# Normalising behind the statistics on ScalarE alone, with logarithm and exponential from one table set

## The chip, the cores and the metric

One core of a Trainium2 chip. The metric is the device time of one execution in microseconds (us); smaller is better. Engines are named as in the profile: PE is TensorE, PEld its weight loads, DVE VectorE, ACT ScalarE, POOL GpSimd, SP SyncE. Each engine works through its own instruction queue strictly in order; a wait at the head of a queue holds everything behind it.

## The reference, cut to what matters

A graph network of four layers over 6250 nodes with 64 features and 206250 edges (sorted by destination). Per layer, with `msg` an edge's message:

```
msg  = relu(h[src] + edge_attr) + 1e-7
ex   = exp(msg*t - segment_max(msg*t)[dst])
agg  = segment_sum(msg * ex / segment_sum(ex)[dst])
z    = relu(layernorm((h + agg) @ w1 + b1))        # 128 wide: norm 1
h    = h + z @ w2 + b2
next = relu(layernorm(h))                          # 64 wide: norm 2
layernorm(x) = (x - mean) * rsqrt(var + 1e-5) * g + b
```

## The kernel before, in words

`prepare` and the stages after it encode the edges and lay them out (up to 1750 us of the trace). Then `layer` runs three times in a loop (tag `mid`) and once more (tag `last`).

A layer walks over 49 blocks `d` of 128 nodes. The edges of a block lie in slots, one edge of each of the 128 nodes per slot: 32 slots whose source rows come by matmuls with one-hot matrices (`passes`, L1273), and `S.V[d]` more (6 to 39) whose rows POOL gathers from `ztab` with one indirect DMA per slot (`gathers`, L1258). For each block DVE adds both to the encoded edges (`add` L1290, four times; `over` L1302, which waits for the gathers), takes the maximum over slots (`most`, L1309, L1313), subtracts it (`sub`, L1332, two or three slices), ACT takes the exponential (L1338), DVE multiplies (`mul`, L1346), PE sums both over the slots (L1356), and DVE folds the four partial sums (`fold`, L1366).

Odd blocks have many gathered slots, even ones few. Blocks are finished in pairs, (1,2), (3,4) and so on, called units: `node_unit(u)` is a Python generator that issues agg, two matmuls and both norms, cut into steps by `yield`. The order on each queue is set at build time: `steps(n, last)` takes up to `n` steps of the unit between the pieces of the block loop. A `yield "gap"` ends the current call of `steps` early (unless n is 99), so that other work is issued in between. Of one unit, norm 1 is issued from the end of block d (odd) to the adds of d+1, and norm 2 from the first `mul` of block d+1 to the adds and the `over` of d+2.

`norm` (L232 to L265) works on two nodes of a partition at once (columns c = 0, 1): DVE takes statistics (L235, L239) and half the variance (L243), ACT takes `Ln` and `Exp` of [128, 2] for a first root (L246, L248, each with a table load before it), three gaps follow, DVE corrects the root by one Newton step (L253 twice, L257) and forms the shift (L260), and ACT applies both (L263, twice). After norm 2 DVE multiplies and adds the gains (L1439, L1444), then comes L1464 and a chain of ACT casts and DVE subtractions that splits the row in three bf16 parts (L1475, L1479), before POOL writes the row to `ztab` (L1488). In the last layer L1455 and a POOL scatter to the output (L1460) stand in their place, issued within the unit's own step; `fetch_out` (L1525) loads what is added there.

POOL's queue in a layer: at the top of iteration d `gathers(d+1)` (which waits for `over(d-1)`), in the last layer with even d `fetch_out`, then the row writes of finished units.

Of the kernel before, what the change touches and what calls it, by code (L numbers as in the profile page):

```python
# [12 lines left out]
ACT = mybir.ActivationFunctionType  # L13
# [3 lines left out]
LN_EPS = 1e-05  # L17
# [125 lines left out]
def build(nc, S, T):  # L143
    PE, VE, AE, GP, SP = nc.tensor, nc.vector, nc.scalar, nc.gpsimd, nc.sync
# [3 lines left out]
    def sb(name, shape, dt=FP32, ctx=None):  # L148
        return (ctx or top).enter_context(nc.sbuf_tensor(name, shape, dt))

    with top:
# [3 lines left out]
        pe_s, ve_s, ae_s = (next(names) for _ in range(3))  # L155
# [5 lines left out]
        def fresh():  # L161

            return Count(pe_s), Count(ve_s), Count(ae_s)
# [7 lines left out]
        def vwait(value):  # L171
            VE.wait_ge(ve_s, value)
# [22 lines left out]
        mv = sb("mv", [128, 2, 2])  # L195
        nwf = sb("nwf", [128, 8, 2])
        nwi = sb("nwi", [128, 4, 2], I32)

        def rsqrt_steps(V, v, y, f, g, i, w):

            vwait(w)
            k = V(VE.tensor_scalar(i, v.bitcast(I32), 1, None, ALU.logical_shift_right))
            V(VE.tensor_scalar(f, v, -0.5, None, ALU.mult))
            yield
            vwait(k)
            k = V(VE.tensor_scalar(y.bitcast(I32), i, -1, RSQRT_SEED, ALU.mult, ALU.add))
            yield
            for _ in range(3):
                vwait(k)
                if v.shape[-1] == 2:  # L210
                    for c in (0, 1):
                        k = V(VE.scalar_tensor_tensor(g[:, c:c + 1], y[:, c:c + 1],
                                                      f[:, c:c + 1], y[:, c:c + 1],
                                                      ALU.mult, ALU.mult))
                else:
                    k = V(VE.tensor_tensor(g, y, y, ALU.mult))
                    vwait(k)
                    k = V(VE.tensor_tensor(g, g, f, ALU.mult))
                yield
                vwait(k)  # L220
                k = V(VE.scalar_tensor_tensor(y, g, 1.5, y, ALU.add, ALU.mult))
                yield
            return k
# [8 lines left out]
        def norm(V, A, src, width, out):  # L232

            for s in (0, 1):
                q = V(VE.bn_stats(st[:, s, :], src[:, s, 0:width]))  # L235
            yield
            vwait(q)
            for s in (0, 1):
                q = V(VE.bn_aggr(mv[:, s, :], st[:, s, :]))  # L239
            yield  # L240
            vwait(q)
            root, half, by, shift = (nwf[:, i, :] for i in range(4))
            q = V(VE.tensor_scalar(half, mv[:, :, 1], LN_EPS, -0.5, ALU.add, ALU.mult))  # L243

            AE.wait_ge(ve_s, q)
            q = A(AE.activation(by, half, ACT.Ln, scale=-2.0))  # L246
            AE.wait_ge(ae_s, q)
            q = A(AE.activation(root, by, ACT.Exp, scale=-0.5))  # L248
            for _ in range(3):
                yield "gap"  # L250
            VE.wait_ge(ae_s, q)
            for c in (0, 1):
                q = V(VE.scalar_tensor_tensor(by[:, c:c + 1], root[:, c:c + 1], half[:, c:c + 1],  # L253
                                              root[:, c:c + 1], ALU.mult, ALU.mult))
            yield
            vwait(q)
            q = V(VE.scalar_tensor_tensor(root, by, 1.5, root, ALU.add, ALU.mult))  # L257
            yield
            vwait(q)
            q = V(VE.scalar_tensor_tensor(shift, mv[:, :, 0], -1.0, root, ALU.mult, ALU.mult))  # L260
            AE.wait_ge(ve_s, q)
            for s in (0, 1):
                q = A(AE.activation(out[:, s, 0:width], src[:, s, 0:width], ACT.Identity,  # L263
                                    bias=shift[:, s:s + 1], scale=root[:, s:s + 1]))
            return q  # L265
# [44 lines left out]
        def prepare():  # L310

            P, V, A = fresh()
            W = S.CH + 128
            with ExitStack() as pc:
                cst = sb("cst", [128, CONST_COLS - KEEP_COLS], FP32, pc)
                c = {n: cst[:, a - KEEP_COLS:b - KEEP_COLS] for n, (a, b) in CONST.items()
                     if a >= KEEP_COLS}
# [52 lines left out]


                GP.memset(clr[:, :], 0.0).then_inc(e_s, 1)
                k_one = V(VE.memset(one[:, :], 1.0))
                V(VE.memset(zrow[:, :], 0.0))
                PE.wait_ge(ve_s, k_one)
# [249 lines left out]
                for i, a in enumerate(range(0, NB, 512)):  # L625
                    w = min(512, NB - a)
                    if i >= 2:
# [25 lines left out]
                q = V(VE.tensor_copy(ni[:, 0, :], rank))  # L653
# [7 lines left out]
                q = V(VE.scalar_tensor_tensor(tmp[:, :], ni[:, 1, :], 128.0, rank, ALU.mult,  # L661
                                              ALU.add))
# [40 lines left out]
        def sorted_path():  # L703

            with ExitStack() as fc:
# [28 lines left out]
                with nc.Fori(0, S.L - 1) as i:  # L734
                    layer(i, "mid", layer_args)
                layer(S.L - 1, "last", layer_args)

        def lay(z, npd, wri, dci, outi, ovi, yc):
# [461 lines left out]
        def layer(number, tag, args):  # L1200
            (oh, z, h, npd, wri, dci, outi, ovi, xb, gb, mx, top_x, cm, ds, nt, zb, zr) = args
            final = tag == "last"
            P, V, A = fresh()
            lc = ExitStack()
            with lc:
                n_ep, ep_slots = 3, 24
# [167 lines left out]
                def node_unit(u):  # L1374
# [7 lines left out]
                    if u - 1 in k["node", "z"]:  # L1382
# [29 lines left out]
                    yield "linear1"  # L1412
                    VE.wait_ge(pe_s, q)
                    q = yield from norm(V, A, NA[:, 0:256].rearrange("p (s c) -> p s c", s=2),
                                        128, hb)
                    yield "normed"
# [10 lines left out]
                    for s in (0, 1):  # L1427
# [5 lines left out]
                    yield  # L1433
                    vwait(q)
                    q = yield from norm(V, A, h[:, u, :].rearrange("p (s f) -> p s f", s=2), 64,
                                        hb)
                    yield "gap"
# [168 lines left out]
        def general_layers(gs):  # L1606
# [118 lines left out]
            def node_pair(j, cnt, row0, n_io):  # L1725
# [40 lines left out]
                yield  # L1766
                vwait(k_hb)
                q = yield from norm(V, A, hb, 128, hb)
                PE.wait_ge(ae_s, q)
                for s in (0, 1):  # L1770
# [150 lines left out]
            with nc.Fori(0, S.L) as number:  # L1921
# [17 lines left out]
                with nc.Else():  # L1939
                    put_out(V, out_parts)  # L1940

        prepare()
        fast = nc.values_load(flag[0:1, 0:1], min_val=0, max_val=1)
        clear_all()
# [104 lines left out]
```

## Time and profile before

| | |
|---|---|
| median of 3 runs | 6229.18 us (6227.09 to 6238.08) |
| the profiled execution's own time | 6223.69 us |
| its span, first to last instruction | 6219.3 us |
| mean granted TensorE clock | 0.823 |
| busy: DVE, PE, POOL, ACT | 4590.5, 4569.7, 4260.6, 2451.0 us |
| the four layers start at | 1749.9, 2858, 3967, 5075.8 us |

The profile gives for each engine the time in which it was executing. "Idle before" in a row is the time for which the engine stood still before it, with what it waited for behind the arrow. Several executions of an instruction in a row are merged to one line with "x2".

### The profile page before, as it was taken

To read this page: it belongs to the slowest core of one execution; us is meant where nothing else is said; L and a number is where in the kernel's file an instruction comes from. 1 tells how busy PE (TensorE), PEld (TensorE's weight loads), DVE (VectorE), ACT (ScalarE), POOL (GpSimd) and SP (SyncE) were. 2 spreads that over 40 slices of the span, in tenths; PEclk is the share of its full clock that TensorE was granted. 3 is DMA by queue.
4 is the path that set the end of the run, shared out by engine and by line. 5 is a ranking of instruction groups with operands and counts; after the bars stand their busy time and mean duration, and the time that the engine had idled before them with its cause. 6 is when DMAs were issued, how large, how long until landed. Compare 5 with 4: busy or idle time off the path is not lost. (4 is left out here: it accounts for less than half of the span.)

```text
span 6219.3 us, 106998 instructions
## 1 busy us (share of the span) xinstructions
PE 4569.7 (73%) x43557; PEld 3223.3 (52%) x43557; DVE 4590.5 (74%) x7210; ACT 2451.0 (39%) x3848; POOL 4260.6 (69%) x3850
## 2 busy tenths in 40 slices
PE   6715788989937877883877788478878856777776
PEld 6705777888824544452444454245444534444443
DVE  9432555444438999994899999389999948988887
ACT  3403666555513444441334444133443423433333
POOL 3054777766557777774777777477777747777775
PEclk9956988666668998896899889689988978888887
DMA  9962777665565555544555555445555544555452
GB/s 365 416 218 81 255 277 270 230 246 214 190 186 174 177 180 172 185 156 119 169 174 184 176 175 175 119 149 177 180 169 183 183 132 136 172 167 172 158 168 87
DMA packets 323285, 1168.13 MB, mean 188 GB/s; under 512 B 142130, under 2 KB 145380, under 8 KB 255444
## 3 DMA queue, kind: packets, MB, share of 16 engines
q1 hardware_dynamic: 172852, 890.91, 39.1%
q0 software_dynamic: 134800, 214.63, 13.8%
q10 hardware_dynamic: 15120, 55.50, 2.2%
q8 instruction: 352, 5.77, 0.4%
q14 instruction: 161, 1.32, 0.1%
HBM read 910.82 MB, written 249.92 MB: 187 GB/s over the span
## 5 line engine op out<-in xcount | busy, mean ns | idle before, releaser
L1258 POOL DMA_INDIRECT gb<-ztab,ovi x2704 | 2991.3, 1106 | 1009.7 <-issue 826.9
L1356 PE MATMUL bank<-ep_mid,keep 128*128 128x512 f32 (+3 forms) x3474 | 1579.0, 613 | 18.5 <-DVE ep_mid L1346 18.5
L1356 PEld LDWEIGHTS bank<-ep_mid,keep 128*128 128x128 f32 x3474 | 703.8, 204 | 859.3 <-issue 830.2
L1309 DVE TENSOR_REDUCE mx<-xb 128x64 f32<-128x2816 f32 (+17 forms) x196 | 1018.1, 5195 | 3.6
L1273 PE MATMUL bank<-zpw,oh_layers 128*128 128x64 bf16 x28812 | 879.8, 194 | 155.4 <-DMA zpw<-ztab 155.4
L1273 PEld LDWEIGHTS bank<-zpw,oh_layers 128*128 128x128 bf16 x28812 | 874.5, 98 | 210.7 <-DMA zpw<-ztab 156.5
L1096 POOL DMA_INDIRECT ecell<-zpw,ptg x588 | 646.7, 1100 | 227.6 <-issue 177.7
L1404 PE MATMUL bank<-keep,na 128*128 128x128 f32 x100 | 47.5, 475 | 963.1 <-DVE na L1401 963.1
L925 PE MATMUL bank<-byk,zpw 88*88 88x102 f32 (+13 forms) x4608 | 649.5, 327 | 57.8 <-DVE zpw L906 54.1
L925 PEld LDWEIGHTS bank<-byk,zpw 88*88 88x88 f32 (+13 forms) x4608 | 638.0, 229 | 68.9 <-DVE zpw L906 60.3
L1319 ACT ACTIVATE cm<-top_x,nt 128x64 f32<-128x64 f32 x196 | 68.2, 348 | 1505.5 <-DVE top_x L1313 1505.5
L906 DVE TENSOR_TENSOR zpw<-keep,kct 88x440 f32<-88x440 f32 (+13 forms) x468 | 285.3, 631 | 467.4 <-PE bank L925 464.1
L1290 DVE TENSOR_TENSOR xb<-bank,xb 128x512 f32<-128x512 f32 x784 | 510.2, 684 | 107.0 <-PE bank L1273 82.1
L1356 PE MATMUL bank<-ep_last,keep 128*128 128x512 f32 (+3 forms) x1158 | 533.9, 620 | 6.2 <-DVE ep_last L1346 6.2
L1404 PEld LDWEIGHTS bank<-keep,na 128*128 128x128 f32 x100 | 18.2, 182 | 975.4 <-DVE na L1401 975.4
L1338 ACT ACTIVATE ep_mid<-ep_mid,pack 128x1280 f32<-128x1280 f32 (+10 forms) x327 | 444.8, 1390 | 174.9 <-DVE ep_mid L1332 171.7
L1332 DVE SCALAR_TENSOR_TENSOR ep_mid<-xb,top_x 128x1280 f32<-128x1280 f32 (+10 forms) x327 | 484.2, 1527 | 8.8 <-DVE top_x L1313 1.4
L1346 DVE SCALAR_TENSOR_TENSOR ep_mid<-xb,ep_mid 128x1280 f32<-128x1280 f32 (+10 forms) x327 | 489.5, 1524 | 0.5 <-ACT ep_mid L1338 0.5
L1356 PEld LDWEIGHTS bank<-ep_last,keep 128*128 128x128 f32 x1158 | 237.1, 207 | 291.5 <-issue 282.7
L844 ACT COPY bys<-bank 88x325 f32<-88x325 f32 (+11 forms) x468 | 198.6, 424 | 474.6 <-PE bank L925 471.1
L1302 DVE TENSOR_TENSOR xb<-gb,xb 128x768 f32<-128x768 f32 (+17 forms) x196 | 210.5, 1074 | 207.8 <-DMA gb<-ztab,ovi 207.7
L844 ACT COPY byk<-bank 88x512 f32<-88x512 f32 (+10 forms) x306 | 316.0, 1158 | 28.0 <-PE bank L885 27.8
(222 smaller groups left out, 5816.5 us busy)
## 6 DMA issues: line engine op xcount, KB each, us to landing
oh_layers<-ohd SPq DMA_DIRECT2D x196, 1568.0 KB, 9.8
ea_in<-in_ea SPq DMA_DIRECT2D x101, 512.0 KB, 8.4
enc<-es_out ACTq DMA_DIRECT2D x101, 512.0 KB
cb<-rowc SPq DMA_DIRECT2D x49, 1024.0 KB, 5.7
gb<-ztab,ovi POOLq DMA_INDIRECT x2704
ohd<-oh_lay SPq DMA_DIRECT2D x49, 576.0 KB
xb<-ecell SPq DMA_DIRECT2D x20, 1408.0 KB
ohd<-oh_lay SPq DMA_DIRECT2D x49, 512.0 KB
```

What stands on the lines that cost most here:

```text
L844: k["ev"][m] = A(AE.copy(to, src(bank[4 + m % 4])))
L906: k["hot"][g] = V(VE.tensor_tensor(hot[0:kp, g % 3, 0:n, 0:mp], iota1[0:kp, None, 0:mp].broadcast_to([kp, n, mp]), kct[0:kp, a:a + n][:, : ...
L925: q = PE.matmul(b[0:mp, WIDE * j:WIDE * j + WIDE], hot[0:kp, g % 3, j, 0:mp], byk[0:kp, at_d:at_d + WIDE], start=True, stop=True)
L1096: at["sc"][j, h] = sc_l[h](GP.indirect_dma_start(T["ecell"], bass.IndirectOffsetOnAxis(ap=ptg[:, j % 2, e:e + 1], axis=0), prows[:, h, a:a ...
L1258: at["g"][d] = ga_l[d % 2](GP.indirect_dma_start(gb[d % 2][:, 64 * v:64 * v + 64], None, T["ztab"], bass.IndirectOffsetOnAxis(ap=ovi[:, i: ...
L1273: q = PE.matmul(gps[j % n_gp][:, 64 * (s % 8):64 * (s % 8) + 64], oh[:, d % 2, at_oh:at_oh + 128], zp[:, b, 64 * part:64 * part + 64], sta ...
L1290: k["add"][d] = V(VE.tensor_tensor(x, gps[j % n_gp][:, 0:64 * (hi - lo)], x, ALU.add))
L1309: q = V(VE.tensor_reduce(mx[:, 0:64], x_of(d, 0, S.S[d]).rearrange("p (s f) -> p f s", f=64), AX.X, ALU.max))
L1332: k["sub"][d, i] = V(VE.scalar_tensor_tensor(ep[:, r, 0:b - a, 64:128], x_of(d, a, b).rearrange("p (s f) -> p s f", f=64), 0.0, top_x[:, d ...
L1338: k["exp"][d, i] = A(AE.activation(ep[:, r, 0:b - a, 0:64], ep[:, r, 0:b - a, 64:128], ACT.Exp, scale=tcol))
L1346: k["mul"][d, i] = k["mul"][d] = V(VE.scalar_tensor_tensor(ep[:, r, 0:b - a, 64:128], x_of(d, a, b).rearrange("p (s f) -> p s f", f=64), 0 ...
L1356: q = PE.matmul(both[d % 2][:, 0:w], ident, rows[:, 128 * (c - a):128 * (c - a) + w], start=(c == 0), stop=(c + 4 >= S.S[d]), skip_group_c ...
```

## The change

`norm` issues nothing on DVE after the statistics. ACT takes `Ln(var + eps)` with the epsilon as a bias from a constant column, and half the variance and the negative mean as `Identity` with a scale; then `Exp`; then the Newton step and the shift as `Identity` activations on single columns ([128,1]), the second factor given as a per-partition scale (and 1.5 as a per-partition bias). The three gaps and the yields between DVE's steps are gone. At the start of a layer the table set that holds both functions is loaded.

```diff
+        eps = sb("eps", [128, 3])
...
-            root, half, by, shift = (nwf[:, i, :] for i in range(4))
-            q = V(VE.tensor_scalar(half, mv[:, :, 1], LN_EPS, -0.5, ALU.add, ALU.mult))
-
+            root, half, by, shift, less, fix = (nwf[:, i, :] for i in range(6))
             AE.wait_ge(ve_s, q)
-            q = A(AE.activation(by, half, ACT.Ln, scale=-2.0))
+            q = A(AE.activation(by, mv[:, :, 1], ACT.Ln, bias=eps[:, 0:1]))
+            A(AE.activation(half, mv[:, :, 1], ACT.Identity, bias=eps[:, 1:2], scale=-0.5))
+            A(AE.activation(less, mv[:, :, 0], ACT.Identity, scale=-1.0))
             AE.wait_ge(ae_s, q)
             q = A(AE.activation(root, by, ACT.Exp, scale=-0.5))
-            for _ in range(3):
-                yield "gap"
-            VE.wait_ge(ae_s, q)
+            AE.wait_ge(ae_s, q)
             for c in (0, 1):
-                q = V(VE.scalar_tensor_tensor(by[:, c:c + 1], root[:, c:c + 1], half[:, c:c + 1],
-                                              root[:, c:c + 1], ALU.mult, ALU.mult))
-            yield
-            vwait(q)
-            q = V(VE.scalar_tensor_tensor(root, by, 1.5, root, ALU.add, ALU.mult))
-            yield
-            vwait(q)
-            q = V(VE.scalar_tensor_tensor(shift, mv[:, :, 0], -1.0, root, ALU.mult, ALU.mult))
-            AE.wait_ge(ve_s, q)
+                q = A(AE.activation(by[:, c:c + 1], root[:, c:c + 1], ACT.Identity,
+                                    scale=half[:, c:c + 1]))
+            AE.wait_ge(ae_s, q)
+            for c in (0, 1):
+                q = A(AE.activation(fix[:, c:c + 1], by[:, c:c + 1], ACT.Identity,
+                                    bias=eps[:, 2:3], scale=root[:, c:c + 1]))
+            AE.wait_ge(ae_s, q)
+            for c in (0, 1):
+                q = A(AE.activation(root[:, c:c + 1], root[:, c:c + 1], ACT.Identity,
+                                    scale=fix[:, c:c + 1]))
+            AE.wait_ge(ae_s, q)
+            for c in (0, 1):
+                q = A(AE.activation(shift[:, c:c + 1], less[:, c:c + 1], ACT.Identity,
+                                    scale=root[:, c:c + 1]))
+            AE.wait_ge(ae_s, q)
...
+                for i, value in enumerate((LN_EPS, -0.5 * LN_EPS, 1.5)):
+                    V(VE.memset(eps[:, i:i + 1], value))
...
             P, V, A = fresh()
+            AE.preload_act_table_set("natural_log_exp_and_others")
```

## Rows read from the trace of the kernel before

**Rows 1.** Windows, second and fourth layer: us, busy (instructions) by engine, PEclk, DMA share, GB/s

```profile
2858.00:3967.00 1109.00, 814.76 (x8686) 506.20 (x8686) 938.32 (x1365) 418.46 (x657) 805.09 (x725) 0.85 0.51 165
5076.00:6219.00 1143.00, 820.77 (x8686) 507.34 (x8686) 928.81 (x1314) 390.76 (x557) 858.53 (x774) 0.84 0.49 155
```

**Rows 2.** Waits, DVE, second layer: us in total, times, longest

```profile
DVE h L1432 <- PE bank L1428: 36.1, 25, 3.8
...
DVE zr L1479 <- ACT zb L1475: 24.1, 27, 1.0
```

**Rows 3.** Waits, DVE and POOL, fourth layer

```profile
DVE xb L1302 <- DMA gb<-ztab,ovi: 112.0, 20, 34.9
...
POOL out L1460 <- DVE zb L1455: 46.4, 3, 26.6
```

**Rows 4.** Timeline of DVE, norm 2 of one unit, first layer: start, us, what

```profile
2326.49 0.25 DVE L239 BATCH_NORM_AGGREGATE mv<-st 128x2 f32<-128x6 f32 x2
...
2326.84 1.35 DVE L1346 SCALAR_TENSOR_TENSOR ep_mid<-xb,ep_mid 128x1152 f32<-128x1152 f32 x1
...
2328.11 1.28 DVE L1290 TENSOR_TENSOR xb<-bank,xb 128x512 f32<-128x512 f32 x2
...
2331.36 0.29 DVE L1439 TENSOR_TENSOR na<-hb,pack 128x128 f32<-128x128 f32 x1 [0.24 <-ACT hb L263]
...
2331.89 1.22 DVE L1302 TENSOR_TENSOR xb<-gb,xb 128x1024 f32<-128x1024 f32 x1
...
2333.03 0.28 DVE L1464 SCALAR_TENSOR_TENSOR zb<-na,keep 128x128 f32<-128x128 f32 x1
...
2340.12 0.29 DVE L1479 TENSOR_TENSOR zr<-zr,zb 128x128 f32<-128x128 f32 x1 [0.98 <-ACT zb L1475]
2340.33 3.42 DVE L1332 SCALAR_TENSOR_TENSOR ep_mid<-xb,top_x 128x1536 f32<-128x1536 f32 x2
```

**Rows 5.** Groups by shape, ACT: count, busy us, mean ns of one, idle before

```profile
L248 ACT ACT_TABLE_LOAD x200 | 256.6, 1283 | 3.6
L1338 ACT ACTIVATE ep_mid<-ep_mid,pack 128x1536 f32<-128x1536 f32 x117 | 184.5, 1577 | 127.3 <-DVE ep_mid L1332 125.9
...
L263 ACT ACTIVATE hb<-h,nwf 128x64 f32<-128x64 f32 x200 | 77.2, 433 | 220.2 <-DVE nwf L260 220.2
...
L248 ACT ACTIVATE nwf<-nwf 128x2 f32<-128x2 f32 x200 | 40.7, 203 | 2.2
```

**Rows 6.** Timeline of ACT, last layer

```profile
5255.14 0.20 ACT L246 ACTIVATE nwf<-nwf 128x2 f32<-128x2 f32 x1 [2.76 <-DVE nwf L243]
...
5256.66 0.20 ACT L248 ACTIVATE nwf<-nwf 128x2 f32<-128x2 f32 x1
...
5263.53 0.35 ACT L1319 ACTIVATE cm<-top_x,nt 128x64 f32<-128x64 f32 x1 [4.58 <-DVE top_x L1313]
5263.91 0.35 ACT L1322 ACTIVATE cm<-cm,npd 128x64 f32<-128x64 f32 x1
...
5276.64 0.77 ACT L263 ACTIVATE hb<-h,nwf 128x64 f32<-128x64 f32 x2 [1.84 <-DVE nwf L260]
```

**Rows 7.** Waits, ACT, whole span

```profile
ACT yt L1424 <- PE bank L1419: 92.8, 83, 5.7
```

**Rows 8.** Timeline of DVE and ACT, end of the second layer

```profile
3929.77 0.69 DVE L1366 TENSOR_REDUCE ds<-bank 128x128 f32<-128x512 f32 x1 [8.90 <-PE bank L1356]
...
3934.31 0.29 DVE L1385 TENSOR_TENSOR ds<-ds,cm 128x128 f32<-128x128 f32 x1
...
3939.38 0.25 DVE L239 BATCH_NORM_AGGREGATE mv<-st 128x2 f32<-128x6 f32 x2
...
3942.40 0.81 ACT L263 ACTIVATE hb<-bank,nwf 128x128 f32<-128x128 f32 x2 [0.81 <-DVE nwf L260]
```

**Rows 9.** Timeline of POOL and DVE, last layer, block 2

```profile
5177.25 1.65 POOL L1258 DMA_INDIRECT gb<-ztab,ovi  x1 [0.30 <-issue]
...
5187.31 0.29 DVE L1432 TENSOR_TENSOR h<-h,bank 128x128 f32<-128x128 f32 x1 [3.76 <-PE bank L1428]
```

## The prediction

> **What bounds the kernel now.** I read the busy time of each engine by layer first. The change touches only `norm`, which runs in the layers (25 units, two norms each, four times: the x200 of [rows 5]). In the second layer DVE is busy for 938 of 1109 us, POOL for 805, PE for 815, ACT for 418 [rows 1]; the first and third layer lie within 2 us of this. ACT has room, DVE has little. POOL's number hides 0.30 us of issue before each of its 725 instructions, some 215 us: with it POOL is at 1020 of 1109. In the last layer (774 instructions, 859 us busy, 232 of issue) it is at 1091 of 1143.
>
> Next the waits. In the second layer DVE waits at L1432 once in each unit for PE, 1.4 us on average, and at L1479 for a cast, 1 us each [rows 2]. In the last layer it waits 112 us for gathers, of which 34.9 are the first large block; POOL there waits for DVE only in the tail (46.4 us, three times) [rows 3]. So layers 1 to 3 are bound by DVE with a stretch bound by PE, and the last one by POOL.
>
> Last the timeline of one unit (two blocks, some 41 us). From L1432 to the first L1346 of the next odd block DVE has work without a hole. From there to the next L1432 it is PE's queue that counts (L1356, L1273, then the transposes L1419): ACT waits for L1419 in 83 of 100 units [rows 7]. Norm 2 lies in the first stretch, norm 1 in the second.
>
> **The change part by part.**
>
> *DVE work that goes.* L243, two L253, L257 and L260 are gone in each norm, with starts 0.07 to 0.45 us apart, in norm 2 together some 0.7 us. In norm 1 I put the same saving (0.9 with its wait) at nothing where PE ends the stretch, 79 of 96 units outside the tails; in the others, some three in each of layers 1 to 3, it counts: -2.5 us a layer. If PE's cover were gone everywhere, it would be -20 a layer.
>
> *The chain on ACT.* ACT's column price: (1577 - 348)/1472 = 0.835 ns, from 1536 columns [rows 5] and the 0.35 us of 64 columns [rows 6]; both have one pointer operand. With two elements and no pointer an activation takes 0.203. One pointer and one column: 0.35 - 0.05 = 0.295. Two pointers: 0.433 - 0.053 = 0.38 [rows 5]. Two in a row take 0.77 instead of 0.87: they overlap by 0.10. A dependent one starts 0.03 after the end of its source (5263.88, 5263.91) [rows 6]. From the end of L239: 0.03; Ln, half, less and Exp 0.20 + 0.20 + 0.11 + 0.20 = 0.71; the square 0.20 + 0.295, with its handoff 0.53; fix 0.28 + 0.38 + 0.03 = 0.69; root 0.53; shift 0.53. Each 0.53 or 0.69 holds its own handoff. L263 starts at 0.03 + 0.71 + 0.03 + 0.53 + 0.69 + 0.53 + 0.53, about 3.04, and DVE can start L1439 after 0.77 + 0.03, at **3.84 us**. Before, L263 came after 2.77 in a tail, where nothing lies between (3939.63 to 3942.40) [rows 8]: the chain is not shorter without its load, it is 0.27 longer. Bounds: 2.4 us if every small activation took the 0.203 of the cheapest one, 4.5 if none overlapped.
>
> A rule of the Trainium skill bears on this: "ScalarE: Activation LUTs", section "What ACT_TABLE_LOAD costs", puts a switch at 2.66 us, 1.28 for the load and 1.38 for a drain. The trace shows the 1.283, and the Exp starts 1.32 after the end of the Ln (5255.34, 5256.66): no drain. By the page each exposed load taken away would give 1.38 more, 11 us in the eight tail norms, and the time would be 6268. The same section prices an activation at 186 ns + 0.833 a column + 93 for each pointer; by that the chain is an estimated 3.7, and the time again some 10 us lower.
>
> *The wait it makes.* The three gaps are gone too, and this is the main term. After the second slice's L1346, `steps(4)` now meets L1439 at once, where before it stood behind two gaps and all four L1290. DVE waits there for ACT's whole chain, and behind it in DVE's queue stand the four L1290, L1302 and L1309 of the next block; behind those the PE work of that block. L1346 ends about 1.4 after L239, so the stall is about 2.4 us. Before, L1439 started 4.62 after L239 [rows 4]; the mean over a layer's 23 units is 4.69.
>
> From L239's end to L1332, which part differs: before, L1439 at 4.69, then 0.54 to L1302, 0.20 for L1464, and L1479 with its wait and its fellow, 1.37 (2340.12 less 0.98, and 0.2 each). Sum 6.80. After: L1439 at 3.84, L1444 and L1464 0.33 + 0.33 + 0.20, four L1290 at 0.60 (L1290 x2 at 2328.11, 1.28 less an overlap of 0.08) 2.40, two L1479 0.40 without a wait, because their casts now run under an L1290. Sum 7.50. **+0.7 us a unit**, I take 0.75 for the piece that no longer overlaps. Bounds: -0.7 with the chain at 2.4, +1.4 at 4.5. Layers 1 to 3: 23 x 0.75 = +17.3 each.
>
> *Tails.* The last pair's norm 2 before stood behind `fold`, which waits 8.9 us for PE: from L1366's end (3930.46) to L1385 (3934.31) 3.85 us [rows 8]. It now is issued before that wait and is done under it; two L1479 and a cast wait stay, 1.0 us. -2.85, and +0.27 for each of the two exposed norms of the last unit: -2.3. In the last layer it is -2.1 (no L1479).
>
> *Layers 1 to 3:* 17.3 - 2.5 - 2.3 = +12.5 each, **+37.5**. POOL gets more lead, not less.
>
> *The last layer.* There are no L1479, so DVE's own pace worsens more: after L1439 0.86 + 2.40 = 3.26 against 0.74, less 0.85: +1.65 a unit, from 41 (1109 less some 105 of head and tail, over 24.5 units) to 43. POOL's 1091 us over 24.5 units are 44 a unit and would hide it. But L1455 moves too, and its POOL scatter with it: it is issued in the even block's multiplications, now ahead of the gathers of the block after next. In block 2 POOL's last gather ends at 5178.9 and two fetches follow, to 5181.5, while L1432 starts at 5187.3 [rows 9]; L1455 ends 0.96 + 3.84 + 0.66 + 0.3 = 5.8 after that, at 5193.1: POOL, which never waited here, stands 11.7 us. That lead doesn't come back in a layer bound by POOL. Following the last gather of each odd block (the first at 5178.9 [rows 9], 24 in all, 42 to 47 us apart), with 5 to 7 us for landing, I get stalls of 11.7, 0, 0.3, 2.1, 0 and 0.7 and then none: +14.8. With the tail **+12.7**. Bounds: +3 (the lead given back), +35 (a stall in each unit).
>
> *The rest.* One table load a layer, under the start of the layer, where ACT waits for the first maximum; three DVE memsets in `prepare`, under its DMA waits. Nothing, at most 1.3 a layer.
>
> Sum: 37.5 + 12.7 = +50 on the profiled execution's 6223.7, 6274. The median of the runs shown is 5.5 above that execution: **6279 us**.
>
> **The rivals.**
> 1. *The wait is hidden and DVE's saving counts (faster).* The place is L1439. It decides where the chain is under 3.1 us: 0.72 less over 69 units cancels the 50. With the chain at 2.4 us: 69 x -0.7 = -48, tails -9, norm 1 -8, last layer +5, 6169. For it: ACT is idle around all norms and the single-column activations have no row of their own. Against it: three dependent pairs with pointers, each 0.5 by the nearest rows.
> 2. *No change.* The chain at 2.9 to 3.3, or PE's stretch, where norm 1's saving may count more often than I say, taking up the difference: 6229. For it: ACT waits for L1419 only 1.1 us a unit [rows 7], so PE's lead is thin.
> 3. *Table loads stay.* If the preload isn't held across the loop or the Exp of L1338 gets its own set, each norm keeps a load between Ln and Exp: +1.28 on the stall, 3 x 25 x 1.3 + 17 = +115: 6394. Against it: nothing in the rows; both Ln and Exp get a load each time now, which only says that their sets differ.
> 4. *The last layer costs more.* With landing times near 8 us, as for some odd blocks, POOL and DVE wait for each other in turn: (8 + 43 - 2.9 + 44)/2 = 46 against 44 a unit, +25 more: 6304.
>
> **How the numbers follow.** Chances: forecast 0.60, rival 1 0.10, rival 2 0.12, rival 3 0.06, rival 4 0.12. Runs of this kernel tell 0.2% from no change, 12.5 us: faster 0.10; within it rival 2 and a low end of the forecast, 0.15; slower 0.75. An error of 0.3 us in the chain is 21 us, and the last layer's bounds give -10 and +22; the range 6220 to 6312 leaves out most of rival 1 and rival 3.
>
> **What would show it.** DVE waits at L1439 for ACT, 2.4 us in each unit (some 58 us a layer, against 7 before), and no longer 24 us a layer at L1479. ACT's activations on nwf: 0.20 to 0.38 each, 3.0 us from L239 to L263. Four table loads or so in place of 400. The wait at L1432 grows by 0.5 to 0.9 in each unit, since norm 1's saving ends there. POOL waits some 11 us at its first L1460. The second layer takes 1121 us, the last 1156. It is wrong if L1439 waits under 1.5 us, if L1432's wait stays as it was while the layer gets shorter, or if POOL's scatter waits nowhere.

## The result and the profile after

The changed kernel takes 6307.03 us, the median of 4 runs (6290.8 to 6312.98), against 6228.14 (6223.19 to 6238.08) of the kernel before: 1.0127 times its time, 95% interval 1.0102 to 1.0153. It is slower by 79 us, with 6279 forecast.

Lines of the changed kernel have other numbers: `norm` is L236 (statistics), L240 (their aggregate), L245 (Ln), L246 (half), L247 (less), L249 (Exp), L252 (by), L256 (fix), L260 (root), L264 (shift), L268 (apply). Behind it all numbers are 8 higher: L1439 is L1447, L1432 is L1440, L1302 is L1310, L1460 is L1468. In gaps3 they are another 2 higher.

The first part of the page: busy us, share, instructions.

```profile
PE 4572.7 (73%) x43556; PEld 3229.3 (51%) x43557; DVE 4487.6 (71%) x6213; ACT 2423.4 (38%) x5452; POOL 4304.7 (68%) x3850
```

DVE is busy for 103 us less than before and the kernel takes 79 more: the busy time of the fullest engine went the other way than the time. PE's is the same within 3 us; POOL's is 44 higher with the same 3850 instructions.

The profiled run has a span of 6300.5 us (its own time is 6304.69) at the same mean clock, 0.823; the layers start at 1758.4, 2889.3, 4015.7 and 5141.5. So the parts of the +81.2 us of span are: preparation +8.5, layers 1 to 3 +22.8, +17.5 and +16.9, last layer +15.5. The windows that answer to [rows 1]:

```profile
2889.00:4016.00 1127.00, 810.22 (x8686) 504.20 (x8686) 912.30 (x1115) 412.48 (x1058) 817.20 (x725) 0.86 0.50 162
5141.00:6300.00 1159.00, 830.88 (x8686) 512.91 (x8686) 903.58 (x1064) 381.40 (x958) 863.88 (x774) 0.85 0.48 153
```

In the second layer DVE has 26 us less to do and stands still for 44 more. Where, its waits say (us in total, times, longest), to be held against [rows 2]:

```profile
DVE na L1447 <- ACT hb L268: 59.4, 25, 3.8
DVE h L1440 <- PE bank L1436: 49.0, 25, 6.4
DVE xb L1310 <- DMA gb<-ztab,ovi: 40.4, 4, 34.0
...
DVE zr L1487 <- ACT zb L1483: 1.1, 3, 0.4
```

The first row is the new wait: 59.4 us a layer behind ACT. The last shows what it took over: the 24.1 us at the casts are 1.1. The wait for gathers was 34.3 in one piece before, of which nothing changes; the 6 us in three further pieces are new.

One unit, DVE and then ACT (start, us, engine, line, operation; idle time before it in brackets), to compare with [rows 4]:

```profile
4764.63 0.25 DVE L240 BATCH_NORM_AGGREGATE mv<-st 128x2 f32<-128x6 f32 x2
4764.91 1.43 DVE L1354 SCALAR_TENSOR_TENSOR ep_mid<-xb,ep_mid 128x1216 f32<-128x1216 f32 x1
4768.65 0.29 DVE L1447 TENSOR_TENSOR na<-hb,pack 128x128 f32<-128x128 f32 x1 [2.31 <-ACT hb L268]
...
4769.83 0.69 DVE L1298 TENSOR_TENSOR xb<-bank,xb 128x512 f32<-128x512 f32 x1 [0.17 <-issue]
4770.44 0.28 DVE L1487 TENSOR_TENSOR zr<-zb 128x128 f32<-128x128 f32 x1
```

```profile
4764.91 0.29 ACT L245 ACTIVATE nwf<-mv,eps 128x2 f32<-128x2 f32 x1 [1.74 <-DVE mv L240]
...
4765.40 0.19 ACT L249 ACTIVATE nwf<-nwf 128x2 f32<-128x2 f32 x1
4765.61 0.48 ACT L252 ACTIVATE nwf<-nwf 128x1 f32<-128x1 f32 x2
4766.13 0.67 ACT L256 ACTIVATE nwf<-nwf,eps 128x1 f32<-128x1 f32 x2
...
4767.85 0.77 ACT L268 ACTIVATE hb<-h,nwf 128x64 f32<-128x64 f32 x2
```

From the end of L240 (4764.88) to L1447 (4768.65) it is 3.77 us, in each of the 69 units (23 in each of layers 1 to 3) the same within 0.01, where 3.84 was forecast. The 0.46 us from L1472 (4769.37, not shown) to L1298 are not typical: in 66 of the 69 units they are 0.21. DVE has 1.43 us of work to put in front of it and stands for 2.31. Ln and Exp follow each other with no load between. The loads that are left, from the groups of ACT (count, busy us, mean ns):

```profile
L1211 ACT ACT_TABLE_LOAD x4 | 5.1, 1283 | 77.1 <-PEq L169 44.2 <-issue 32.9
```

In the last layer POOL stands at its first scatter, as forecast (11.7 there):

```profile
5258.63 0.99 POOL L1468 DMA_INDIRECT out<-zb,outi  x1 [11.34 <-DVE zb L1463]
```

Four more such waits of 1.4 to 1.6 us follow ahead of the tail, 17.3 in all. The waits of DVE there hold 95.8 us for gathers against the 112.0 of [rows 3]: part of what POOL is late was waiting already.

The tail, to compare with [rows 8]:

```profile
3980.87 0.69 DVE L1374 TENSOR_REDUCE ds<-bank 128x128 f32<-128x512 f32 x1 [5.67 <-PE bank L1364]
3981.48 0.28 DVE L1487 TENSOR_TENSOR zr<-zb 128x128 f32<-128x128 f32 x1
3982.12 0.29 DVE L1487 TENSOR_TENSOR zr<-zr,zb 128x128 f32<-128x128 f32 x1 [0.36 <-ACT zb L1483]
3982.45 0.29 DVE L1393 TENSOR_TENSOR ds<-ds,cm 128x128 f32<-128x128 f32 x1
```

The norm is gone from behind the fold; the wait for PE in front is 3.2 us shorter because the norm now lies in it.

### The profile page after: what moved, and what is told of

It reads as the page before. It is cut to its first block and busy times, and to the rows that moved or that the text cites. A ratio compares the mean times of both kernels' runs of the same rounds, so it can differ in the third digit from the quotient of the medians.

```text
span 6300.5 us, 107708 instructions
## 1 busy us (share of the span) xinstructions
PE 4572.7 (73%) x43556; PEld 3229.3 (51%) x43557; DVE 4487.6 (71%) x6213; ACT 2423.4 (38%) x5452; POOL 4304.7 (68%) x3850
## 5 line engine op out<-in xcount | busy, mean ns | idle before, releaser
L1266 POOL DMA_INDIRECT gb<-ztab,ovi x2704 | 3033.5, 1122 | 1043.8 <-issue 833.1
L1317 DVE TENSOR_REDUCE mx<-xb 128x64 f32<-128x2816 f32 (+17 forms) x196 | 1014.3, 5175 | 6.7
L1298 DVE TENSOR_TENSOR xb<-bank,xb 128x512 f32<-128x512 f32 x784 | 498.6, 682 | 115.3 <-PE bank L1281 95.1
L1346 ACT ACTIVATE ep_mid<-ep_mid,pack 128x1280 f32<-128x1280 f32 (+10 forms) x327 | 444.8, 1390 | 157.6 <-DVE ep_mid L1340 154.4
L1310 DVE TENSOR_TENSOR xb<-gb,xb 128x768 f32<-128x768 f32 (+17 forms) x196 | 209.9, 1071 | 206.7 <-DMA gb<-ztab,ovi 206.7
```

Source lines behind the costliest of these rows:

```text
L1266: at["g"][d] = ga_l[d % 2](GP.indirect_dma_start(gb[d % 2][:, 64 * v:64 * v + 64], None, T["ztab"], bass.IndirectOffsetOnAxis(ap=ovi[:, i: ...
L1298: k["add"][d] = V(VE.tensor_tensor(x, gps[j % n_gp][:, 0:64 * (hi - lo)], x, ALU.add))
L1317: q = V(VE.tensor_reduce(mx[:, 0:64], x_of(d, 0, S.S[d]).rearrange("p (s f) -> p f s", f=64), AX.X, ALU.max))
L1346: k["exp"][d, i] = A(AE.activation(ep[:, r, 0:b - a, 0:64], ep[:, r, 0:b - a, 64:128], ACT.Exp, scale=tcol))
```

## The experiments

The profiled runs differ in how long preparation takes (below), so I compare profiles from the first gather of layer 1 to the end. That stretch stands in the last column, behind the ratio of all runs to the kernel before on the same chip. The runs were on four chips, where the kernel before has medians of 6228.14, 6221.41, 6223.18 and 6218.92 us, so medians of two kernels can differ by up to 9 us by the chip alone.

```
                 median us (runs)  ratio (95%)                 first gather to end
before           6221 (12)         -                           4470.4
after            6307 (4)          1.0127 (1.0102 to 1.0153)   4543.0
gaps3            6248 (6)          1.0035 (1.0023 to 1.0048)   4489.9
before_preload   6209 (7)          0.9976 (0.9964 to 0.9989)   4458.8
late_scatter     6294 (4)          1.0116 (1.0099 to 1.0133)   4532.8
no_preload       6406 (2)          1.0296 (1.0275 to 1.0316)   4648.1
filled_after     6295 (4)          1.0126 (1.0105 to 1.0148)   4548.1
split            6230 (11)         1.0017 (1.0008 to 1.0026)   4476.6
before_no_gaps   6380 (4)          1.0261 (1.0246 to 1.0277)   4618.9
fewer_before     6091 (2)          0.9790 (0.9761 to 0.9819)   4311.6
fewer_after      6158 (2)          0.9898 (0.9878 to 0.9918)   4385.4
fewer_gaps3      5990 (2)          0.9629 (0.9609 to 0.9648)   4214.1
```

Below, stretch 1 runs from the start of L1440 (DVE) in a unit to the start of L1415 (ACT) in the next (norm 2 lies in it) and stretch 2 from there to L1440 (norm 1). Sums are over the 23 units of a layer between its head and tail, means of layers 1 to 3.

**gaps3: the gaps put back, behind the last activation.** This asks whether the engine or the place in DVE's queue costs the time.

```diff
                 q = A(AE.activation(out[:, s, 0:width], src[:, s, 0:width], ACT.Identity,
                                     bias=shift[:, s:s + 1], scale=root[:, s:s + 1]))
+            for _ in range(3):
+                yield "gap"
             return q
```

> The changed kernel with one thing put back: three gaps, now behind the whole chain on ScalarE (after L263's successors, before norm returns). All arithmetic stays on ScalarE, no table loads. My theory (the time was lost because DVE meets L1439 before ScalarE is done): the wait at L1439 falls from 2.3 to about 0.5 us a unit, L1479 stays without a wait, the last layer's scatter goes back behind the gathers; layers 1 to 3 some 25 us shorter than before the change, where POOL's gathers become the bound, the last one 3 shorter: about 6150 us. Rival (the chain on ScalarE costs by itself, through later exponentials or through PE's clock): it stays at 6228 or above.

It took 6248.27 us, 59 less than the change (53 from the first gather to the end) and still 0.35% more than before. By its time that is where I had put the rival (6228 or above), and far from my 6150. The stall is gone as expected; DVE in one unit:

```profile
4724.29 0.29 DVE L1449 TENSOR_TENSOR na<-hb,pack 128x128 f32<-128x128 f32 x1 [0.52 <-ACT hb L268]
...
4730.17 1.16 DVE L1312 TENSOR_TENSOR xb<-gb,xb 128x960 f32<-128x960 f32 x1 [4.47 <-DMA gb<-ztab,ovi]
```

But in its place stands a wait to which the expectation gave far too small a price. The waits of DVE in the second layer:

```profile
DVE xb L1312 <- DMA gb<-ztab,ovi: 78.2, 14, 35.7
...
DVE na L1449 <- ACT hb L268: 15.8, 24, 3.8
```

Of the 44 us that the stall gives back (59.4 less 15.8), 38 go into the wait for gathers (78.2 less 40.4). DVE is now quick enough that POOL's queue bounds layers 1 to 3 too.

**fewer_before, fewer_after, fewer_gaps3: that floor lowered.** Every fourth gather is left out of the same three kernels (`gb` is cleared once a layer).

```diff
+                        if v % 4 == 1 and v < S.V[d] - 1:
+                            continue
```

> The kernel before with every fourth gather of a block left out (its slots keep old or zero rows, so the sums aren't the reference's), POOL a fifth less loaded; the two gather buffers are cleared at each layer's start. It makes DVE and PE the bound in all four layers. Layers 1 to 3 lose only the shorter wait at the second block, 10 us each, the last comes down to the same 1100: about 6150.

> The changed kernel with the same gathers left out (the sums aren't the reference's). If the wait at L1447 is the cost by itself: 23 units of +1.0 us, less 6 for norm 1 and 3 for the tail in layers 1 to 3 (+14 each) and +1.65 a unit in the last (+30): about 75 us above fewer_before. If the loss was mostly in POOL's longer gathers: under 40 above it.

> gaps3 with the same gathers left out (the sums aren't the reference's). My theory now (in gaps3 DVE became faster than before, but POOL's gathers are the floor and grew longer): with POOL out of the way it is about 100 us below fewer_before (30 in each of layers 1 to 3, 14 in the last). Rival (the chain on ScalarE costs in some other place): it stays 20 to 30 above fewer_before, as gaps3 stood to before.

They took 6090.67, 6157.76 and 5990.27. The first was forecast at 6150; its last layer came down to 1047 us, and not only to 1100. The change costs 67 us here as well (75 forecast), and its stretch 1 is 22.5 us a layer longer, with no wait for gathers in it: 0.98 us a unit is what the new order and the smaller work cost together in DVE's queue. With the gaps back the same arithmetic is 100 us faster than before, as forecast, and not 20 to 30 slower as the rival had it.

27.5 us a layer of this lie in stretch 1. They are not all work moved to ACT: DVE's busy time there falls by 13.1 us, and the wait at the casts, 22.6 us a layer in fewer_before, is gone, which is a matter of where the casts are issued; the wait at L1451 takes 6.6 us back and short pauses the rest. (L1451 is L1447 of the changed kernel.) The table loads are gone too, worth some 13 us in all (before_preload, below). No run has the old arithmetic with the casts issued in this place, so how much of the 100 us an order alone would have brought is not shown. In the full kernel gaps3 has the same gains in stretch 1, and 35.5 us a layer of waits for gathers there outweigh them.

**before_no_gaps: the other half of the question.** The kernel before, with its norm on both engines, without the three gaps.

```diff
-            for _ in range(3):
-                yield "gap"
```

> The kernel before with its three gaps taken out and nothing else: arithmetic, engines and table loads as they were. If the order of issue is what costs, and not the engine, it loses too: DVE waits 1.7 us at L253 for Ln, load and Exp in both norms; in norm 2 a wait of 0.98 at L1479 goes in return, in norm 1 some 1.2 us of slack takes part of it: 15 to 45 us a layer, 6221 + 100 = about 6320. If the work on ScalarE is what costs: within 20 us of 6221.

It took 6379.68 us, 161 more than before, where I had forecast 100. DVE stands at the head of its queue for Exp:

```profile
DVE nwf L251 <- ACT nwf L248: 89.3, 50, 1.8
```

Stretch 1 is 29 us a layer longer and stretch 2 26. Nothing but the place of issue differs from before, so the order alone is worth two times what the change cost. In stretch 2 I had counted on 1.2 us of slack ahead of PE; with a DVE stall of 1.8 us in it, each unit takes 1.1 more. The last layer, where POOL is the bound, is 9.9 us shorter instead (1132.8 for 1142.7): the same stalls cost nothing there, and POOL's gathers in it are shorter, 1083 ns on average for 1116.

**no_preload: what the loads do once the chain is exposed.**

```diff
-            AE.preload_act_table_set("natural_log_exp_and_others")
```

> The changed kernel without its preload line. If each norm gets its loads back: one of 1.28 us stands between Ln and Exp in the chain and lengthens the wait at L1447 by the same in each unit, 3 x (23 x 1.28 + 2.6) and some 15 us in the last layer, 6307 + 110 = 6417. Rival (the load runs beside the half and less activations or is hoisted): under 6330.

It took 6406.27 us, 99 more than the change (105 from the first gather to the end). The loads are back, 400 of them, and the wait at L1447 (L1446 here) grows by 1.42 us a unit:

```profile
L249 ACT ACT_TABLE_LOAD x200 | 256.6, 1283 | 3.5
```

```profile
DVE na L1446 <- ACT hb L268: 94.9, 25, 5.3
```

This would have been rival 3; its 6394 from the load's own 1.28 is 12 short, its mechanism right.

**before_preload: the same line alone on the kernel before.**

```diff
             P, V, A = fresh()
+            AE.preload_act_table_set("natural_log_exp_and_others")
```

> The kernel before with the preload line alone, norm as it was. My theory (the loads were hidden but for the two norms in each layer's tail and 1 us or so of waits at L253): 4 x (2.6 + 1.2) = 15 us less than before, 6213. Rival (a switch costs a drain beyond the load, or loads held back the exponentials of L1338): 6150 or less. Rival (nothing exposed at all): 6228.

6208.54 us, ratio 0.9976: 396 loads, 508 us of ACT's busy time (256.6 twice, less 5.1), are worth 12.9 us, 0.24%, because the gaps already hid nearly all of them: stretch 1 and stretch 2 are the same within 0.2 us a layer, and what shows lies in the tails, where the last unit's stretch 2 falls from 8.6 to 7.3. It is the fastest kernel here that does the whole work, and the one part of the change to keep.

**late_scatter: the scatter of the last layer set back.**

```diff
+                        for _ in range(4):
+                            yield "gap"
```

placed between the end of the unit's arithmetic (L1463) and POOL's scatter to the output.

> The changed kernel; in the last layer alone the scatter to the output (L1468) is issued four gaps after its data, so that it stands behind the gathers of the block after next again, as before the change. Layers 1 to 3 are untouched. My theory (POOL's wait at the first scatters shifts the whole last layer): the last layer 12 us shorter than the changed one's 1159, 6295 in all. Rival (the last layer loses by DVE's and PE's slower pace, the order on POOL's queue doesn't matter): 6307, no difference.

6294.26 us. The early waits at the scatter are gone, two in the tail are left:

```profile
POOL out L1470 <- DVE zb L1463: 39.2, 2, 22.2
```

The last layer, from its first gather, is 10.6 us shorter (1147.6 for 1158.2). So about two thirds of its +15.5 come from POOL standing at the scatter. The intervals of the two ratios (1.0127 and 1.0116) overlap, so this rests on the profiles.

**split: norm 1 from the changed kernel, norm 2 from the one before.**

```diff
-                    q = yield from norm(V, A, h[:, u, :].rearrange("p (s f) -> p s f", s=2), 64,
+                    q = yield from norm_dve(V, A, h[:, u, :].rearrange("p (s f) -> p s f", s=2), 64,
```

(`norm_dve` is the old function; the preload stays.)

> Norm 1 as in the changed kernel (all on ScalarE, no wait of DVE in it), norm 2 as before (Newton step on DVE, three gaps), table set loaded once. My theory: of the two norms only norm 1 is worth moving; it takes 8.5 us out of the later units' stretch to L1440 and adds 3 in the earlier ones, 5.5 in each of layers 1 to 3, on top of what the single table load brings in the tails (12 to 15): 6221 - 12 - 17 = 6192. Rival (POOL's gathers have no slack for it, they grow as in gaps3): no better than 6208, which the preload alone gave.

6229.62 us against 6218.92, ratio 1.0017: slower, not faster, where I had forecast 6192; the rival (no better than 6208) came. Norm 1's saving ends at PE; the waits of DVE in the second layer:

```profile
DVE h L1475 <- PE bank L1471: 56.0, 25, 6.4
DVE xb L1345 <- DMA gb<-ztab,ovi: 39.5, 2, 35.3
```

The first row was 36.1: it takes up the 20 us that DVE got, and stretch 2 of the later units stays at 229.2 us (230.1 before). Against before_preload, which has the load line too, moving norm 1 costs some 25 us (1.0017 less 0.9976, of 6220), 18 from the first gather to the end. Of that, 3.8 us in the second layer's wait for gathers are seen (39.5, and 35.7 in before_preload). Split also drops norm 1's gaps, and this experiment doesn't separate that from the arithmetic.

**filled_after: more work for PE.** Stretch 2 of the later units (12 to 23) got 8.8 us a layer shorter by the change and that of the earlier ones (1 to 11) 2.3 longer. In both, a part runs at the lower of TensorE's two clock levels (1.2 in place of 2.4 GHz), so I asked whether the clock sets them.

```diff
+                    if d % 2:
+                        for _ in range(6):
+                            PE.matmul(NB[:, 256:512], ident, b1, start=True, stop=True,
+                                      skip_group_check=True)
```

> The changed kernel with six matmuls more on PE in each odd block, after its passes, into an unused part of a bank, where PE otherwise has nothing to do for 7 us. If the clock that PE is granted after that idle time is what makes the stretch to L1440 longer in the first ten units of a layer (20.3 us where later ones take 18.3): 15 us a layer less, about 6250. Rival (those stretches are long by their own work): 6307 or, where the extra matmuls hold up the transposes, more.

6295.29 us. From the first gather on it is 5 us longer than the change. The extra matmuls stand in stretch 1. There the time at the lower level falls from 131 to 92 us a layer, and the stretch doesn't get shorter (528.9, then 530.1): DVE sets its pace, not PE. In stretch 2, about which I asked, that time hardly moved, so the missing gain says nothing against the clock. The profiles themselves settle it. For stretch 2: its length, the time at the lower level in it, and the length less half of that time (what it would take at the higher level throughout), in us a layer:

```
                 units 1 to 11            units 12 to 23
before           213.5   38.6   194.2     230.1   57.0   201.6
after            215.8   43.2   194.2     221.3   40.5   201.0
filled_after     214.4   40.4   194.2     223.6   45.4   200.9
split            214.1   39.9   194.2     229.2   56.8   200.8
gaps3            214.7   41.0   194.2     227.4   46.3   204.3
before_no_gaps   222.5   45.2   199.9     247.3   52.1   221.2
```

In the early units the third number is 194.1 or 194.2 in each of the four layers of eleven profiles; only before_no_gaps, with its DVE stall, has more. So stretch 2 there lasts as long as PE's own work at the clock it is granted, and what DVE has to do in norm 1 doesn't count. The +2.3 us of the early units is all clock, and of the -8.8 of the later ones 8.2. One later unit, before and after the change (the third value from the end is the granted clock):

```profile
3534.99:3554.29 19.30, 18.87 (x184) 11.49 (x184) 17.76 (x23) 8.81 (x13) 15.31 (x14) 0.89 0.39 115
```

```profile
3578.55:3596.86 18.31, 17.88 (x184) 11.12 (x184) 17.10 (x18) 7.88 (x20) 14.83 (x12) 0.93 0.39 116
```

PE does the same 184 matmuls and is busy in all but 0.43 us of either. Before, 4.43 us of it are at the lower level, after 2.45: half of the difference is the 0.99 us that it got shorter. Its longest piece:

```profile
3536.45 11.94 PE L1356 MATMUL bank<-ep_mid,keep 128*128 128x512 f32 x24
```

```profile
3580.01 10.96 PE L1364 MATMUL bank<-ep_mid,keep 128*128 128x512 f32 x24
```

In split the same unit has 4.45 us at the lower level and takes 19.31, so norm 1 alone isn't what moved the clock. PE stood idle for 7.59 us ahead of it before, 8.58 after and 7.58 in split; why the higher level comes sooner after the change stays open. The clock also doesn't explain why early units take longer than later ones: without the lower level they still take 17.7 and 16.8 us each.

## Why the prediction was right, and where its sizes were off

**The side and the mechanism.** Slower was forecast with 0.75, and the time lies within the range, 5 us from its upper end. Of the signs named, these came: the wait at L1439 (58 us a layer forecast, 59.4 measured), the casts' wait gone, activations of 0.19 to 0.38 us, 2.97 us from the end of the statistics to the first L263 (3.0 forecast), four table loads, the wait at L1432 longer by 0.52 a unit (0.5 to 0.9), 11.34 us at POOL's first scatter (11.7). gaps3 and before_no_gaps, not the rows alone, show that the place of issue makes the loss.

**Layers 1 to 3: +19.1 each, forecast +12.5.** By terms, in the order of the prediction:

- *The unit*, +17.3 forecast (0.75 each), +22.7 measured (0.99), and 22.5 with the gathers out of the way. The chain itself was mis-sized by 0.07 only. Its sum left out that Ln and the half read their bias through a pointer and take 0.30 and 0.28 us, not 0.20; as each starts 0.2 us after the one before it, this didn't show. What was missed lies behind the chain, in small pieces: L1452 to L1472 takes 0.39 us where I had 0.33, and from L1310, the maximum L1317 and L1321 DVE reaches its next instruction 0.12, 0.06 and 0.11 us later than before (means of fewer_before and fewer_after), where less is left to overlap with.
- *Gathers*, 0 forecast ("POOL gets more lead, not less"), about +6 a layer. This is the step that failed. POOL does get ahead, but `gathers(d+1)` waits at the top of the iteration for `over(d-1)`, and there it stands now:

```profile
L1266 POOL DMA_INDIRECT gb<-ztab,ovi x2704 | 3033.5, 1122 | 1043.8 <-issue 833.1 <-DVE xb L1310 111.7 <-POOLq L169 77.8
```

  `gathers` waits on nothing else of DVE, so the 52.3 us under L1464 in the row of the kernel before (below; L1464 follows L1302 at once) are this wait too. With 23.8 under L1302 itself it was 76 us there, and 112 now. Lead that a buffer doesn't hold is lost. In the second layer these waits grew from 21.6 to 34.4 us, and DVE finds POOL late at blocks 37, 41 and 45. The gathers are also longer, 1122 ns on average against

```profile
L1258 POOL DMA_INDIRECT gb<-ztab,ovi x2704 | 2991.3, 1106 | 1009.7 <-issue 826.9 <-POOLq L169 76.7 <-DVE zb L1464 52.3
```

  and 1130 in gaps3:

```profile
L1268 POOL DMA_INDIRECT gb<-ztab,ovi x2704 | 3055.8, 1130 | 983.9 <-issue 837.1 <-POOLq L169 77.2 <-DVE xb L1312 24.7
```

  In the second layer that is 16 ns for each of 676 gathers, 11 us of POOL's time, about as much as the 13 us of lead lost. Which of the two makes the waits isn't separated.
- *Norm 1*, -2.5 forecast; -6.5 measured (+2.3 in the early units, -8.8 in the later). That the sign agrees is luck: the term stood for DVE's saved work, split shows no gain from that in these stretches, and the shifts are the granted clock, for which the sum had no term.
- *Tails*, -2.3 forecast; -3.1 for the last pair and +0.3 for each exposed norm, -2.5.

These give 22.7 + 6.1 - 6.5 - 2.5 = +19.8, 0.7 us over what the layers show.

**The last layer: +15.5, forecast +12.7.** The new waits at the scatter are 17.3 us for 14.8. But "POOL, which never waited here" was wrong: one of the three waits in [rows 3] is an early one, 5.04 us at 5195.73, so the net is 12.2. late_scatter bears out the mechanism with 10.6 us. Where the remaining 5 or so come from isn't shown.

**Preparation: +8.5, not forecast.** It isn't the change's arithmetic. In this profile PE runs at the lower clock level for 27 us from 14.1 us on, and the first gather comes at 1757.5; in filled_after, with the same preparation, it does so for 7 us from 12.0 on, and the gather comes at 1743.6. Its first 60 us, after and then filled_after (the third value from the end is the granted clock):

```profile
0.00:60.00 60.00, 49.02 (x244) 42.00 (x245) 50.19 (x129) 16.66 (x31) 12.66 (x11) 0.74 0.61 226
```

```profile
0.00:60.00 60.00, 43.53 (x289) 37.85 (x290) 50.16 (x129) 19.51 (x37) 12.66 (x11) 0.91 0.74 283
```

The low start also occurs without the change's memsets (before_no_gaps, 0.74). Six of the eight profiles with the memsets have it and one of the four without; whether they make it likelier, these are too few to say. Leaving out the fewer_ kernels, which also clear `gb` before the first gather, that gather comes at 1755.2 to 1760.0 in the five profiles with the low start and at 1743.6 to 1753.2 in the four without.

**The rivals.** Rival 1 needed a chain under 3.1 us; it is 3.77. Rival 2 named PE's thin lead as what might let norm 1's saving count: split's wait at L1475, 20 us longer, shows the opposite. Rival 3 is no_preload, not the change. Rival 4 (+25 in the last layer) didn't come: after the first, the early waits at the scatter are 1.4 to 1.6 us.

## What to carry to other kernels

Moving small work off the fullest engine pays only if the place where that engine takes the result back moves too: here the changed order made the kernel 67 to 79 us slower, and with a quarter of the gathers left out the same activations with three gaps behind them take 100 us less than the old norm, part of it by casts that no longer hold DVE up. Before putting down a gain for a relieved engine, work out the next floor, here POOL's queue with its two gather buffers, by giving it the new pace; and don't credit lead that a buffer can't hold. Table loads on an engine with room are nearly free when its consumer waits behind other work (13 us for 396) and when it doesn't, each adds its own time and a little more to the exposed wait (1.42 us for 1.28, 99 us in all). In a stretch that PE's own work fills, look at the granted clock before crediting a change of its length to the work that was moved.

## What the runs showed of the hardware

**Small activations.** With no pointer operand and two columns 0.19 us; one column costs 0.287 with one pointer (two columns 0.28 to 0.30) and 0.380 with two:

```profile
L256 ACT ACTIVATE nwf<-nwf,eps 128x1 f32<-128x1 f32 x400 | 133.1, 380 | 6.7
L264 ACT ACTIVATE nwf<-nwf 128x1 f32<-128x1 f32 x400 | 96.0, 287 | 6.5
```

**A table load is 1.28 us and nothing more is seen.** In no_preload, ACT around one load:

```profile
3460.16 0.19 ACT L247 ACTIVATE nwf<-mv 128x2 f32<-128x2 f32 x1
3460.36 1.28 ACT L249 ACT_TABLE_LOAD   x1
3461.66 0.20 ACT L249 ACTIVATE nwf<-nwf 128x2 f32<-128x2 f32 x1
```

The Trainium skill ("ScalarE: Activation LUTs", section "What ACT_TABLE_LOAD costs") adds a drain of 1.38 us. Here the activation in front ends at 3460.35, the load starts at 3460.36 and the Exp at 3461.66: no drain, and the measurement decides.

**A gather's issue on POOL stretches beside some work of DVE.** One gather takes 0.94 us on POOL; POOL and then DVE after the change:

```profile
3590.18 0.94 POOL L1266 DMA_INDIRECT gb<-ztab,ovi  x1 [0.30 <-issue]
3591.43 1.68 POOL L1266 DMA_INDIRECT gb<-ztab,ovi  x1 [0.30 <-issue]
...
3594.75 2.01 POOL L1496 DMA_INDIRECT ztab<-zb,wri  x1 [0.30 <-issue]
```

```profile
3585.35 4.85 DVE L1317 TENSOR_REDUCE mx<-xb 128x64 f32<-128x2752 f32 x1
...
3590.53 3.09 DVE L1340 SCALAR_TENSOR_TENSOR ep_mid<-xb,top_x 128x1536 f32<-128x1536 f32 x2
...
3594.15 1.75 DVE L1354 SCALAR_TENSOR_TENSOR ep_mid<-xb,ep_mid 128x1536 f32<-128x1536 f32 x1
```

Counted over layers 2 and 3 of the kernel before, by what DVE did in the first 0.94 us of the gather: of 485 gathers beside L1332 or L1346, 268 take over 1.1 us. Of 104 beside L1302 and neither of these, 17 do (42 of 105 after the change). Of the other 763, 371 of them beside the maximum L1309 and 201 beside L1290 (one source in PSUM), none does. The Trainium skill ("SBUF — State Buffer", section "Who interferes with whom") says that a VectorE instruction with two SBUF inputs contends with a GpSimd instruction that reads SBUF, and that a reduction never does; for the long instructions these counts agree: L1332, L1346 and L1302 have two such inputs. Short ones (0.3 us, L1401 for one) have them too; 77 of the other gathers stand beside such a one, and the longest takes 0.98 us. That the gather counts as reading SBUF, by its row numbers `ovi`, is inferred. From before to after, the gathers of these two layers grew by 22 us in all: 13 beside L1302, 6 beside the other two. It was not tried to move them.

**What the lower clock level costs.** Where PE's own work fills a stretch, each microsecond at the lower level makes it half a microsecond longer: the 194.2 us above, in eleven profiles with 36 to 48 us a layer at that level. Where DVE sets the pace, 40 us less of it changed nothing (528.9 and 530.1).
